# Biases moved into the last row of the weights, tiles that end with an expert's last row, and tables waited for one by one

## The reference

```python
# FFN: mixture of 16 experts, top 2
logits = xt @ Wg.T + bg
top_vals, top_idx = top_k(logits, 2);  rw = softmax(top_vals)
gu = xt @ Wgu[e] + bgu[e]              # 128 -> 256, gate and up
gate = min(gate, 7); up = clip(up, -7, 7)
gated = (up + 1) * gate * sigmoid(1.702 * gate)
out_e = gated @ Wd[e] + bd[e];  out = sum over the two experts of rw * out_e
# attention: 16 heads of 8, causal, 256 tokens
qkv = x @ W_attn + b_attn; ...; y @ W_proj + b_proj
```

## Time and profile before

| what | value |
|---|---|
| median of three runs | 763.55 us |
| profiled execution, its own time | 764.87 us |
| its span, first to last instruction | 763.0 us |
| TensorE busy | 526.7 us (69%) |
| VectorE busy | 524.5 us (69%) |
| ScalarE busy | 316.6 us (41%) |
| GpSimd busy | 297.4 us (39%) |
| mean granted TensorE clock | 0.867 |

### The profile page before, as it was taken

The page is one execution under the profiler, slowest core; times in us unless marked ns, Lnnn a source line. Parts: engine busy times, 40 slices in busy tenths (PEclk is TensorE's granted clock), DMA queues, the critical chain, the costliest instruction groups (busy, mean ns, idle before and its releaser), DMA issues.

```text
span 763.0 us, 19935 instructions
## 1 busy us (share of the span) xinstructions
PE 526.7 (69%) x6287; PEld 352.4 (46%) x6287; DVE 524.5 (69%) x2691; ACT 316.6 (41%) x602; POOL 297.4 (39%) x308
## 2 busy tenths in 40 slices
PE   3357629999747979788888977888832049999200
PEld 2234218887523546454544544555421038888100
DVE  6865418888777787678767776789746038888722
ACT  1001018888514545445444544334401048888000
POOL 2777750021441424141414102017777200057774
PEclk9999999999969898999899989788965569999755
DMA  9533134455465261435234333301112325566522
GB/s 270 149 97 94 52 96 117 139 161 155 150 208 181 69 194 57 135 119 165 87 112 141 124 100 113 111 2 53 50 48 83 97 65 144 147 171 183 149 80 62
DMA packets 112611, 90.27 MB, mean 118 GB/s; under 512 B 12357, under 2 KB 104970, under 8 KB 112266
## 3 DMA queue, kind: packets, MB, share of 16 engines
q1 hardware_dynamic: 78218, 59.77, 26.0%
q0 software_dynamic: 8192, 16.79, 7.9%
q10 hardware_dynamic: 26112, 12.59, 5.6%
HBM read 44.98 MB, written 44.11 MB: 117 GB/s over the span
## 4 chain that ended last, share of the span: by engine, by line
PE 43%; DVE 21%; issue 13%; POOL 11%; SPq 4%; ACT 3%; DMA 3%; DVEq 1%; ACTq 0%; POOLq 0%
PE banks L1537 10%; POOL by_token L505 8%; DVE by_token L789 5%; PE banks L1548 4%; PE banks L1525 3%; POOL rows_by_expert L543 3%; PE banks L1453 3%; SPq L408 3%; PE banks L1311 2%; PE banks L1501 2%; PE banks L1287 2%; PE banks L1261 2%; DVE x_resident L739 2%; DVE by_token L916 2%; PE banks L1445 2%
## 5 line engine op out<-in xcount | busy, mean ns | idle before, releaser
L789 DVE CUSTOM_DVE_ANT_0 by_token<-banks,konst_sb 128x128 f32<-128x128 f32 (+1 forms) x512 | 147.0, 352 | 29.2 <-issue 28.8
L543 POOL DMA_INDIRECT rows_by_expert<-by_token,posi x120 | 116.2, 968 | 57.2 <-issue 35.0
L1537 PE MATMUL banks<-xT,pT 128*64 128x128 f32 x1536 | 109.3, 286 | 33.6 <-ACT pT L710 17.7
L710 ACT ACTIVATE pT<-w_experts 128x384 f32 x192 | 90.0, 515 | 77.5 <-DMA tab<-tabc 61.9
L610 ACT ACTIVATE pT<-banks 128x1536 f32<-128x1536 f32 x64 | 92.8, 1449 | 54.2 <-PE banks L1289 54.2
L1537 PEld LDWEIGHTS banks<-xT,pT 128*64 128x64 f32 x1536 | 85.5, 141 | 50.6 <-ACT pT L710 33.9
L505 POOL DMA_INDIRECT by_token<-results_by_tile,tilepos x64 | 61.2, 957 | 95.7 <-DMA results_by_tile<-ysb 76.7
L505 POOL DMA_INDIRECT yg<-results_by_tile,tilepos x64 | 61.9, 967 | 75.6 <-DMA results_by_tile<-ysb 57.2
L1124 DVE SCALAR_TENSOR_TENSOR sig<-banks,sig 128x256 f32<-128x256 f32 x96 | 40.4, 421 | 48.6 <-ACT sig L720 47.7
L1548 PE MATMUL banks<-pT,gT 128*64 128x128 f32 x768 | 59.4, 276 | 4.5 <-DVE ysb L1141 4.5
L604 ACT ACTIVATE mT<-banks 128x256 bf16<-128x256 f32 x64 | 24.5, 383 | 90.5 <-PE banks L1236 90.3
(11 more groups left out here) (160 smaller groups left out, 1077.5 us busy)
## 6 DMA issues: line engine op xcount, KB each, us to landing
xt<-rows_by_expert SPq DMA_DIRECT2D x192, 64.0 KB
results_by_tile<-ysb ACTq DMA_DIRECT2D x96, 128.0 KB
q_stack<-q_by_part SPq DMA_DIRECT2D x8, 1024.0 KB, 7.5
k_stack<-k_by_part SPq DMA_DIRECT2D x8, 1024.0 KB, 6.3
q_by_part<-q_parts SPq DMA_DIRECT2D x16, 384.0 KB, 3.4
k_by_part<-k_parts SPq DMA_DIRECT2D x16, 384.0 KB, 2.8
rows_by_expert<-zeros SPq DMA_DIRECT2D x65, 64.0 KB
x_resident<-in_x SPq DMA_DIRECT2D x8, 256.0 KB, 5.4
```

The costliest lines, as they stand in the source:

```text
L543: pool.indirect_dma_start(out=rows_dram, out_offset=bass.IndirectOffsetOnAxis(ap=posi[:, c:c + 1], axis=0), in_=rows_of(f, q)[:, i, :], in ...
L710: last = nc.scalar.activation(w_tile[:, 2 * k + i, :], w_all[:, bass.ds(held[key][k % 2 * 2 + i], EW)], ACT.Identity)
L789: last = nc.vector.tensor_tensor_reduce(masked[:, (3 * g + qt) * P:(3 * g + 2 * qt + 1) * P], of, lag, 1.0, NEG * NEG_BELOW, ALU.add, ALU. ...
L1537: last = nc.tensor.matmul(bank[2 + k % 2][h * HALF:(h + 1) * HALF, at:at + P], w_tile[:, 2 * k + i, which * F + h * HALF:which * F + (h + ...
```

## The change

1. Wherever a normalised row is written, only its first 127 channels are; channel 127 is set to 1.0 once. Each weight matrix that takes such rows (`wg`, gate/up, q/k/v) has its row 127 replaced by the bias, and row 127 of the original is subtracted from rows 0 to 126. To that end rows 0 to 126, the bias row, and the old row 127 repeated over 127 partitions (`wg_last`, `gu_last`, `w_in_last`) are loaded by separate DMAs. VectorE does the subtraction: one for `wg`, one for attention's weights in quad 2, four for the gate/up weights (4 experts each) in quads 3 to 6.
2. `column_sums`, `spread`, `share`, `bg`, `bqk` and the bias product in `values` are gone; `split_biases` works on one row of 128.
3. Tiles end with an expert's last row. Every region of rows has 128 pad rows ahead of it; one DMA zeroes the pads of all 32 regions once. `zrow` and `zero_tiles` are gone, and a second small count product is added.
4. `copy_weights` and `evac_y` wait for their own pass's table only.

```diff
-            sp.dma_start(wg[:, :], w_g).then_inc(s_const, 16)
-            sp.dma_start(bg[:, :], b_g.partition_broadcast(P)).then_inc(s_const, 16)
+            sp.dma_start(wg[0:LAST, :], w_g[0:LAST, :]).then_inc(s_const, 16)
+            sp.dma_start(wg[LAST:C, :], b_g).then_inc(s_const, 16)
+            sp.dma_start(wg_last[:, :], w_g[LAST:C, :].rearrange("a e -> (a e)").partition_broadcast(LAST)).then_inc(s_const, 16)
...
-            sp.dma_start(w_of_expert[:, :, 0:2 * F], w_gu.rearrange("p (e w) -> p e w", e=E)).then_inc(s_wexp, 16)
+            sp.dma_start(bias_in[:, :], b_proj).then_inc(s_bias3, 16)
+            sp.dma_start(w_of_expert[0:LAST, :, 0:2 * F], w_gu[0:LAST, :].rearrange("p (e w) -> p e w", e=E)).then_inc(s_wexp, 16)
+            sp.dma_start(gu_last[:, :], w_gu[LAST:C, :].rearrange("a w -> (a w)").partition_broadcast(LAST)).then_inc(s_wexp, 16)
+            sp.dma_start(w_of_expert[LAST:C, :, 0:2 * F], b_gu.rearrange("(o e) w -> o e w", o=1)).then_inc(s_wexp, 16)
+            sp.dma_start(w_in[0:LAST, :], w_attn[0:LAST, :]).then_inc(s_watt, 16)
+            sp.dma_start(w_in[LAST:C, :], b_attn.rearrange("(o a) c -> o (a c)", o=1)).then_inc(s_watt, 16)
+            sp.dma_start(w_in_last[:, :], w_attn[LAST:C, :].rearrange("a w -> (a w)").partition_broadcast(LAST)).then_inc(s_watt, 16)
             sp.dma_start(w_of_expert[:, :, 2 * F:EW], w_d.rearrange("p (e w) -> p e w", e=E)).then_inc(s_wexp, 16)
             sp.dma_start(w_of_expert[:, :, EW:WB], b_d.rearrange("e c -> (e c)").partition_broadcast(P).rearrange("p (e c) -> p e c", e=E)).then_inc(s_wexp, 16)
+            sp.dma_start(w_out[:, :], w_proj).then_inc(s_watt, 16)
+
+            sp.wait_ge(s_pool, 1)
+            sp.dma_start(rows_dram[0:SIDES * E * REGION, :].rearrange("(r w) c -> w r c", w=REGION)[0:P, :, :],
+                         zeros[:, :].unsqueeze(1).to_broadcast([P, SIDES * E, C])).then_inc(s_zero, 16)
...
             def table_of(p):
                 g = p % SIDES
-                sp.wait_ge(s_ends, p + 1)
-                sp.dma_start(tab[0:1, g, 2 * TILES:TABW], zrow[:, :]).then_inc(s_tab_ends, 16)
-                sp.wait_ge(s_tab_ends, 16 * (p + 1))
-                if p == 0:
-                    sp.wait_ge(s_pool, 1)
-                    sp.dma_start(rows_dram[0:P, :], zeros[:, :]).then_inc(s_zero, 16)
-                zero_tiles(sp, g)
...
+                def adjust_attention():
+                    dve.wait_ge(s_watt, 64)
+                    nc.vector.tensor_tensor(w_in[0:LAST, :], w_in[0:LAST, :], w_in_last[:, :], ALU.subtract).then_inc(s_asetup, 1)
...
                 def adjust(n):
-                    w_of = w_all.rearrange("p (e w) -> p e w", e=E)
-                    dve.wait_ge(s_fix, n + 1)
-                    nc.vector.tensor_tensor(w_of[:, 2 * n:2 * n + 2, 0:2 * F], bank[6 + n % 2].rearrange("p (n w) -> p n w", n=2),
-                                            w_of[:, 2 * n:2 * n + 2, 0:2 * F], ALU.add).then_inc(s_fixed, 1)
+                    w_of = w_all.rearrange("p (e w) -> p e w", e=E)[0:LAST, 4 * n:4 * n + 4, 0:2 * F]
+                    dve.wait_ge(s_wexp, 80)
+                    nc.vector.tensor_tensor(w_of, w_of, gu_last[:, n * 8 * F:(n + 1) * 8 * F].rearrange("p (e w) -> p e w", e=4),
+                                            ALU.subtract).then_inc(s_fixed, 1)
...
                         read_logits(q)
                         top2(q)
+                        if q == 1:
+                            split_biases()
+                        if q == 2:
+                            adjust_attention()
+                        if 3 <= q < 7:
+                            adjust(q - 3)
                         read_ranks(q)
                         positions(q)
                         if q == 0:
                             spread_of(3)
-                        if q == 1:
-                            split_biases()
...
-                    if p % SIDES == 0 and isinstance(t, int) and (t, k) == (0, 0):
-                        act.wait_ge(s_tab, 32 * (p + 2))
+                    if isinstance(t, int) and (t, k) == (0, 0):
+                        act.wait_ge(s_tab, 32 * (p + 1))
```

More of the change, by code:

```diff
@@ L38 @@
 TILES = TSIDE * TOPK + E
-TABW = 2 * TILES + E
+TABW = 2 * TILES
+LAST = C - 1
 UNROLL = 8
@@ L46 @@
 EW = 2 * F + C
-BW = 2 * F
 WB = EW + C
@@ L247, in build_block @@
         spare = sb("spare", [P, 1])
+        gu_last = by_token[0:LAST, 0:E * 2 * F]
+        wg_last = rest[0][0:LAST, 0:E]
+        w_in_last = rest[0][0:LAST, E:E + 3 * C]
         a_yg = sb("yg", [P, QUAD * TOPK, C])
@@ L403, in stack_rest @@
                     stack_pair(sp, t, half)
[L405 to L408, removed]
         @block.sync
@@ L473, in _ @@
                 table_of(first)
-                sp.wait_ge(s_zero, 16 * (1 + E * (first + 1)))
+                if f == 0:
+                    sp.wait_ge(s_zero, 16)
                 sp.wait_ge(s_scat[0], 16 * TOPK * TSIDE * (f + 1))
@@ L592, in high @@
                 beyond_first(act, a_spread[which], x * 48)
-                nc.scalar.activation(parts[which][:, 0, :], bank[at][:, :], ACT.Identity, bias=bqk[:, which:which + 1]).then_inc(a_high[which], 1)
+                nc.scalar.activation(parts[which][:, 0, :], bank[at][:, :], ACT.Identity).then_inc(a_high[which], 1)
             def evac_v(x, half, at=7):
@@ L767, in normalise @@
                 beyond_first(dve, a_Tp, x)
+                if isinstance(x, int) and x == 0:
+                    nc.vector.memset(xa[:, :, LAST:C], 1.0)
                 for i in range(QUAD):
-                    last = nc.vector.tensor_scalar(xa[:, i, :], row(x, i), a_mv[:, i, 0:1], a_rs[:, i:i + 1], ALU.subtract, ALU.mult)
+                    last = nc.vector.tensor_scalar(xa[:, i, 0:LAST], row(x, i)[:, 0:LAST], a_mv[:, i, 0:1], a_rs[:, i:i + 1], ALU.subtract, ALU.mult)
                 last.then_inc(a_xn, 1)
@@ L776, in split_rest @@
                 beyond_first(dve, a_low[which], x)
-                nc.vector.scalar_tensor_tensor(out=rest[which][:, :], in0=bank[at][:, :], scalar=bqk[:, which:which + 1],
-                                               in1=parts[which][:, 0, :], op0=ALU.add, op1=ALU.subtract).then_inc(a_rest[which], 1)
+                nc.vector.tensor_tensor(rest[which][:, :], bank[at][:, :], parts[which][:, 0, :], ALU.subtract).then_inc(a_rest[which], 1)
             def row_max(t, s):
@@ L1186, in values @@
                         last = nc.tensor.matmul(bank[at][h * HALF:(h + 1) * HALF, i * C:(i + 1) * C], xaT[:, i * P + h * HALF:i * P + (h + 1) * HALF],
-                                                w_in[:, 2 * C:3 * C], start=False, stop=i == QUAD - 1)
+                                                w_in[:, 2 * C:3 * C], start=i == 0, stop=i == QUAD - 1)
                 last.then_inc(a_v, 1)
@@ L1457, in ranks @@
                 def ranks(q):
-                    if q == 0 and f == 0:
-                        pe.wait_ge(s_setup, 3)
                     pe.wait_ge(s_mask, f * NQ + q + 1)
@@ L1481, in counts @@
                 def counts(p):
-                    nc.tensor.matmul(bank[6][0:E, 0:P], macc[:, before(QSIDE * (p % SIDES + 1) - 1) + 1, :], ones[:, :], start=True, stop=True).then_inc(s_count, 1)
+                    nc.tensor.matmul(bank[6][0:E, 0:P], macc[:, before(QSIDE * (p % SIDES + 1) - 1) + 1, :], ones[:, :], start=True, stop=True)
+                    nc.tensor.matmul(bank[6][:, P:P + E], ones[:, :], macc[:, before(QSIDE * (p % SIDES + 1) - 1) + 1, :], start=True, stop=True).then_inc(s_count, 1)
                     pe.wait_ge(s_ntile, p + 1)
@@ L1490, in _ @@
                     units()
-                def column_sums(n):
-                    if n == 0:
-                        pe.wait_ge(s_wexp, 48)
-                        pe.wait_ge(s_bias3, 48 + 48)
-                    if n >= 2:
-                        pe.wait_ge(s_fixed, n - 1)
-                    for i in range(2):
-                        o, e = bank[6 + n % 2][:, i * 2 * F:(i + 1) * 2 * F], 2 * n + i
-                        nc.tensor.matmul(o, share[0:3, :], bias3[0:3, e * BW:e * BW + 2 * F], start=True, stop=False)
-                        last = nc.tensor.matmul(o, spread[:, :], w_all[:, e * WB:e * WB + 2 * F], start=False, stop=True)
-                    last.then_inc(s_fix, 1)
                 for q in range(f * MERGED, NQ + 1):
@@ L1511, in _ @@
                         counts(0)
-                    if f == 0 and q > NQ - E // 4:
-                        column_sums(2 * (q - 1 - NQ + E // 4))
-                        column_sums(2 * (q - 1 - NQ + E // 4) + 1)
-                if f == 0:
-                    pe.wait_ge(s_fixed, E // 2)
                 for p in ((1,), (2, 3))[f]:
```

87 lines of the change are left out of this document (34 added, 53 removed).

## The result

The changed kernel takes 861.38 us (median of 4 runs, 858.98 to 863.23), against 763.92 us for the kernel before on the same chip: a ratio of 1.1277, 95% interval 1.1242 to 1.1311. The profiled execution has a span of 858.6 us, 95.6 more than before.

A forecast was written before the change was run, and what follows sets the result against it. TensorE bounds the passes, something else the stretches ahead. Loads landing at 210 us plus 38.9 start pass 0 137.5 later; second half -28.6, attention -1.5: net +107.4, span 870.4, plus 0.6 gives 871 us, range 843 to 900.

The forecast's parts named there:

- One engine for 127 rows: Weight loads at the start: six DMAs of 127 rows all go to the same one DMA engine, 22 to 25 GB/s.
- T: Start of the kernel: moment at which all loads have landed, forecast at 210 us, bounds 190 to 222.
- SyncE's issue would stand still: SyncE's queue during loading: a stopped SyncE adds only the table's and zeros' issue; beyond the range in 0.04.
- From T to pass 0: First router after the landing: sum, rest of the quads, tables and first product take 38.9 us, so pass 0 starts at 248.9.
- The added sums fill the waits for the ranks: VectorE in the router: sums of 1.25 us go into rank waits of 1.2 each; 0.3 us taken for all.
- Second half: From table 2 to pass 2: rows issued sooner, pass 2 starts at 591.4 instead of 620.0, a gain of 28.6 us.
- Attention: Attention loses eight bias products of 0.6 us: a gain of 0 to 4.8 us, taken as 1.5.
- spread after all: Rival for the loads at the start: 127 rows use 16 engines, landing ends at 37 us, time 699 us; chance 0.09.

The follow-up runs named there:

- e1: Changed kernel with all six loads of 127 rows cut into 112 + 15 rows: 701.52 us, ratio to the kernel before 0.9157.
- e2: Changed kernel with only the two large loads (gate/up weights and `gu_last`) cut into 112 + 15 rows, the four small ones kept at 127: 714.86 us.
- e3: Changed kernel with the load of `gu_last` issued from ScalarE's queue instead of SyncE's: 859.78 us, one run.
- e4: Changed kernel, loads still of 127 rows, with VectorE's five sums and their waits moved behind table 1: 845.67 us.
- e5: e1 with sums in landing order: own semaphore for gate/up loads, their four sums in quads 2 to 5, attention's in quad 6; 691.89 us, ratio to before 0.9053.
- e7: Kernel before with part 3 alone (tiles end with an expert's last row, pads zeroed once): 731.85 us, ratio 0.9584.
- e10: Kernel before without the bias product in `values`, repeat of e9 where before took 763.39 us: 759.76 us, ratio 0.9954.
- e6: e1 with part 4 undone, so weight copies and VectorE wait for both tables of a half again: 707.95 us.
- e9: Kernel before without the bias product in `values`, in a round where before took 930.73 us: 928.89 us, ratio 0.9988.

## Why the prediction was right

Forecast 871 us, range 843 to 900, measured 861.4.

- **One engine for 127 rows: right, and shown.** The profile has the single stream at 24 to 27 GB/s, e1 removes it by the row count alone, the packet counts of e1 and e2 give one engine for 127 rows, and e3 shows that loads of two queues meet on the same one. The Trainium skill ("DMA: Bandwidth & Descriptors", "Why a DMA increments its semaphore by 16 and not by 1") says both, the one engine and that it is the lowest-numbered and so always the same; the runs agree, with e3 for the second half, which the trace of before could not show. Which number it has no view shows.
- **T = 210: measured 205.7.** The large loads went at 24 and 27 GB/s, so 87 and 77 us by the bytes, where I had 87 and 81; the gate/up load's last packets are at 104, where I had 102. That SyncE's issue would stand still for most of the time I had only as a side remark; that it moved nothing in the changed kernel, as the engine's own order puts all behind anyway, fits T but was not tested. It decided e4.
- **From T to pass 0: 38.9 forecast, 37.8 measured.** Quads of 6.1 us and free sums, 1.22 us each against 1.25 forecast. "The added sums fill the waits for the ranks" is shown in e5, where 0.24 us of a wait is left.
- **Second half: -28.6 forecast, -27.8 measured.** Right by its steps.
- **Attention: -1.5 forecast, -8.7 between the two profiles.** This is the term that was mis-sized, and the largest part of the 11.8 us by which the forecast of the span was high (5.4 from T and what follows it, 7.2 here, -0.8 from the second half). The stretch from pass 0 to table 2 is 473.2 and 472.3 us in the two profiles without the new biases (before, e7), and in the nine with them 462.9 to 470.3, mean 466.5: 6 us less, with a scatter of 4 up and down. So 8.7 was one profile's gain, and the steady part is near 6. Leaving out the bias product alone gave 3.5 (2.1 to 4.9) in e10; I had bounded it by 4.8 and taken 1.5. My sum had no term for the granted clock, though, and that moved too. The stretch before and after (columns as in the earlier trace rows):

```profile
111.45:584.64 473.19, 383.80 (x4845) 246.53 (x4845) 362.69 (x2018) 231.65 (x394) 152.97 (x158) 0.88 0.37 114
243.46:707.97 464.51, 371.36 (x4838) 241.90 (x4838) 361.70 (x2023) 229.56 (x394) 176.52 (x181) 0.90 0.39 119
```

TensorE's busy time falls by 12.4 us. The eight products that are gone are at most 4.8 of it, and the rest goes with a granted clock of 0.90 instead of 0.88. So how the 6 us divide between the products' own time, the clock and the sum without a bias operand in `split_rest` is open, and whether the missing products raised the clock as well.
- **The rival "spread after all"** was given 699 us. e1 made it true and measured 701.5. I had 37 us for the landing and it was 43; why was not separated.
- **The parts:** part 3 alone -32.7, parts 1 and 2 alone with cut loads -21.8, all three with the old table waits -56.6 (e6 against before), part 4 another -6.4 (e1 against e6), the loads of 127 rows +160, the sums' order -9.6.

## What to carry to other kernels

Count the rows of each transfer before its bytes: here one row fewer than 128 put 2 MB on one engine of sixteen, and cutting the loads into 112 + 15 took the kernel from 861 to 702 us. A slow transfer stops more than those who wait for its data: whatever is issued behind it in the same queue (here the tables, a bias row) waits too. Where sums for later stages are put into waits of an in-order engine, each should wait for its own data and stand where that has landed.

## What was not expected of the hardware

- The issue of a DMA behind a load on one engine stood for 87.66 us (93.92 with scatters beside it), although that load itself took 0.84 us to issue; a row of 1.5 KB stood for 41.87.
- In e3 two queues shared the one engine by turns, 33 packets each in 20 us, and a packet of 16 KB against one of a few bytes counted alike: 0.54 MB against 0.00 MB.
- In one round of runs the kernel before took 930 us instead of 764, and the profile of e9 in that round has 36% of the chain in waits for nothing that the profile shows, at a mean granted clock of 0.81. The record has the same chip number for it as for the next round, where before took 763 us. Its cause stays open.
